# Attention kernel: value products of a group of heads moved into one run behind the last exponential

## The reference, cut to what matters

```
for 8 images of 512 tokens, width 256, 16 heads, latent width 32:
q_lat, k_lat, v_lat = projections of x to 32 latents a head; rotary on q_lat, k_lat
q_for_k = q_lat @ wqk.T + b
att = softmax(causal(q_for_k @ k_lat.T * 32**-0.5))     # 512 x 512 a head
y = (att @ v_lat) @ l2o.T + b ;  x = layernorm(x + y @ cproj.T + b)
# then: a soft mixture of 16 experts over 64 slots each, residual, layernorm
```

## Time and profile before

| | |
|---|---|
| runs | 1212.70, 1214.39, 1215.88 us; median 1214.39 |
| span of the profiled execution | 1212.4 us |
| TensorE matmul busy | 1152.4 us, 95% |
| VectorE, ScalarE, POOL busy | 769.8 (63%), 667.7 (55%), 596.1 (49%) |
| mask on POOL [L699] | 128 times, 748 ns in the mean |
| value products [L1439] | 1024 matmuls |

### The profile page before, as it was taken

How to read it: one execution, slowest core, us unless ns; L and a number is a source line. 1 busy time by engine, 2 the same in 40 slices (tenths; PEclk the granted TensorE clock), 3 DMA queues, 4 the chain that set the end, 5 groups by cost and what they waited for, 6 DMA issues and landing times.

```text
span 1212.4 us, 19086 instructions
## 1 busy us (share of the span) xinstructions
PE 1152.4 (95%) x6838; PEld 900.5 (74%) x6870; DVE 769.8 (63%) x1250; ACT 667.7 (55%) x946; POOL 596.1 (49%) x400
## 2 busy tenths in 40 slices
PE   6799999999999999998799999988999999999996
PEld 5566666666666666656688888867888888889885
DVE  5778796969686878654667667754544545522444
ACT  2456456665656565647779777755555555630112
POOL 6456565565656565612666666663444444440000
PEclk8799999999999999989899999998999999999998
DMA  4546454556555463630144335356654455364761
GB/s 142 125 111 155 95 132 94 145 120 158 124 127 147 99 161 89 184 108 1 53 157 157 122 122 183 105 165 234 183 166 148 160 163 182 113 213 144 246 234 53
DMA packets 126670, 170.29 MB, mean 140 GB/s; under 512 B 47041, under 2 KB 77186, under 8 KB 126594
## 3 DMA queue, kind: packets, MB, share of 16 engines
q1 hardware_dynamic: 124498, 168.74, 48.2%
q10 hardware_dynamic: 2096, 0.56, 0.2%
HBM read 72.26 MB, written 37.75 MB: 91 GB/s over the span
## 4 chain that ended last, share of the span: by engine, by line
PE 87%; DVE 6%; issue 2%; DMA 2%; ACT 1%; POOL 1%; SPq 1%; ACTq 1%; another core or an unknown queue 1%; DVEq 0%; POOLq 0%
PE ring L431 12%; PE ring L433 11%; PE ring L432 11%; PE ring L1428 7%; PE ring L1578 7%; PE tail L1439 7%; PE ring L1413 6%; PE tail L431 4%; PE tail L432 4%; PE tail L433 4%; PE ring L1461 2%; PE tail L1399 2%; PE tail L1578 2%; PE ring L1415 2%; PE ring L1515 2%
## 5 line engine op out<-in xcount | busy, mean ns | idle before, releaser
L1131 DVE TENSOR_REDUCE mx<-ring 128x4 f32<-128x512 f32 (+2 forms) x192 | 199.3, 1044 | 89.4 <-PE ring L1415 73.1
L842 ACT ACTIVATE pt<-ring 128x1024 f32<-128x1024 f32 (+1 forms) x192 | 169.1, 881 | 117.9 <-PE ring L1428 117.8
L699 POOL TENSOR_SCALAR_AFFINE_SELECT pt<-pt 128x512 f32<-128x512 f32 x128 | 95.7, 748 | 215.1 <-ACT pt L842 215.1
L1413 PE MATMUL ring<-qks 96*128 96x384 f32 (+3 forms) x512 | 137.0, 357 | 7.1 <-DMA qks<-stg 4.8
L1428 PE MATMUL ring<-qks 98*128 98x256 f32 (+3 forms) x512 | 137.5, 372 | 5.8 <-DMA qks<-mts 4.1
L1428 PEld LDWEIGHTS ring<-qks 98*128 98x128 f32 x512 | 79.4, 194 | 71.7 <-issue 47.6
L716 POOL TENSOR_TENSOR dl<-e,dh 128x1024 fp32r<-128x1024 f32 x32 | 76.6, 2404 | 94.6 <-ACT e L913 94.6
L740 POOL TENSOR_TENSOR hl<-hid,hh 128x512 fp32r<-128x512 f32 x64 | 82.7, 1303 | 76.8 <-ACT hh L948 76.8
L1439 PE MATMUL tail<-pt,va 128*32 128x512 f32 (+3 forms) x1024 | 97.0, 451 | 6.6 <-issue 4.9
L1413 PEld LDWEIGHTS ring<-qks 96*128 96x128 f32 x512 | 92.7, 199 | 12.6 <-issue 5.1
L1249 DVE SCALAR_TENSOR_TENSOR hid<-ring,bias_e,gate 128x512 f32<-128x512 f32 x64 | 47.9, 748 | 81.5 <-ACT gate L942 52.2
(11 more groups left out here) (241 smaller groups left out, 3069.7 us busy)
## 6 DMA issues: line engine op xcount, KB each, us to landing
qks<-stg SPq DMA_DIRECT2D x384, 128.0 KB, 2.4
c_dram<-c2s SPq DMA_DIRECT2D x32, 512.0 KB, 5.0
c<-c_dram SPq DMA_DIRECT2D x32, 512.0 KB, 6.5
sl_dram<-sls SPq DMA_DIRECT2D x32, 256.0 KB, 3.4
wg<-in_wg SPq DMA_DIRECT2D x16, 512.0 KB, 5.7
wu<-in_wu SPq DMA_DIRECT2D x16, 512.0 KB, 6.4
wd<-in_wd SPq DMA_DIRECT2D x16, 512.0 KB, 7.1
sl<-sl_dram SPq DMA_DIRECT2D x16, 512.0 KB, 4.6
```

The lines of the kernel that those rows point to most:

```text
L699: nc.gpsimd.affine_select(out=m, in_=m, compare_op=ALU.is_ge, fill=0.0, base=0, pattern=[[0, GH], [1, P]], channel_multiplier=-1).then_inc ...
L842: nc.scalar.activation(pt[j % 2][:, h:h + heads, 0:n], heads_of(tile, heads, n), ACT.Exp, scale=SCALE).then_inc(empty, 1)
L1131: nc.vector.tensor_reduce(out=mx[:, g, h:h + heads, i], in_=heads_of(tile, heads, (i + 1) * P), axis=AX.X, op=ALU.max).then_inc(empty, 1)
L1413: nc.tensor.matmul(scores[:, h, :], qks[0:KS_ROWS, g, 0, h0 + h, i * P:(i + 1) * P], qks[0:KS_ROWS, g, 1, h0 + h, 0:n], start=(h == k), st ...
```

## The change

The value products of a group, which were issued one by one behind the exp units of their blocks, are all given the due time of the last exp unit (`PV_WITH`), so they follow each other. Exp units are spaced by 1.0 instead of 8/6 (`EXP_SLOTS`), masks with them. Every key block has a `pt` buffer of its own: `pt0` of 512 columns a head, `pt1` of 384, `pt2` of 256, `pt3` of 128; `pt2` lies where a gap and two constants lay, which move to the end. The computation is the same. The diff:

```
--- before.py
+++ after.py
@@ -29,7 +29,9 @@
 MAX_UNITS = ((0, 0, 4), (1, 0, 4), (2, 0, 2), (2, 2, 2), (3, 0, 2), (3, 2, 2))
 EXP_UNITS = ((0, 0, 2), (0, 2, 2), (1, 0, 2), (1, 2, 2), (2, 0, 4), (3, 0, 4))
 EXP_LAST = (1, 3, 4, 5)
+PV_WITH = (3, 3, 3, 3)
 UNIT_SLOTS = GROUP_SLOTS / len(MAX_UNITS)
+EXP_SLOTS = 1.0
 
 
 PE_AT = {"lat": -20.25, "wqk": -9.25, "max": 0.0, "neg": 11.0, "exp": 13.25, "v": 14.55, "pv": 15.75, "yT": 28.75, "yTT": 53.5, "cproj": 58.5, "wv": -12.2, "seT": 6}
@@ -51,14 +53,22 @@
             if name in ("lat", "wqk", "neg", "yT", "khi", "qhi", "y", "shuffle", "cos", "qlo", "negmax", "sin", "add", "klo", "stack", "place"):
                 for g in range(G):
                     add(SPAN * b + GROUP_SLOTS * g, (name, b, g))
-            elif name in ("max", "exp"):
+            elif name == "max":
                 for g in range(G):
                     for u in range(len(MAX_UNITS)):
                         add(SPAN * b + GROUP_SLOTS * g + UNIT_SLOTS * u, (name, b, g, u))
-            elif name in ("pv", "mask"):
+            elif name == "exp":
+                for g in range(G):
+                    for u in range(len(EXP_UNITS)):
+                        add(SPAN * b + GROUP_SLOTS * g + EXP_SLOTS * u, (name, b, g, u))
+            elif name == "mask":
                 for g in range(G):
                     for j in range(NT):
-                        add(SPAN * b + GROUP_SLOTS * g + UNIT_SLOTS * EXP_LAST[j], (name, b, g, j))
+                        add(SPAN * b + GROUP_SLOTS * g + EXP_SLOTS * EXP_LAST[j], (name, b, g, j))
+            elif name == "pv":
+                for g in range(G):
+                    for j in range(NT):
+                        add(SPAN * b + GROUP_SLOTS * g + EXP_SLOTS * EXP_LAST[PV_WITH[j]], (name, b, g, j))
             elif name in ("seT", "seh", "sel"):
                 for c in range(NC if b == 0 else 0):
                     add(0, (name, b, c))
@@ -194,15 +204,14 @@
     stg = [place(f"stg{i}", [P, 4, T], f32r) for i in range(2)]
     qks = place("qks", [P, G, 2, GH, T], f32r)
     mts = [place(f"mts{i}", [2 * GH * NT, P], f32r) for i in range(2)]
-    at[0] += 3 * KB
-    identb = place("identb", [P, P], bf16)
-    maskb = place("maskb", [P, GH, P], bf16)
+    pt2 = place("pt2", [P, GH, T - 2 * P], f32)
+    at[0] += 256
     wq = place("wq", [P, P], f32)
     bwq = place("bwq", [P, 1], f32)
     bv = place("bv", [P, C], f32)
     va = place("va", [P, NT, H, L], f32)
     temp_at = at[0]
-    pt = [place(f"pt{i}", [P, GH, T], f32) for i in range(2)]
+    pt = [place("pt0", [P, GH, T], f32), place("pt1", [P, GH, T - P], f32), pt2, place("pt3", [P, GH, P], f32)]
     ys = place("ys", [P, T], f32)
     ytok = place("ytok", [P, NT, C], f32)
     yT_ = place("yT_", [P, NC, T], f32)
@@ -231,6 +240,8 @@
     m2 = place("m2", [P, NS], f32)
     es = place("es", [P, NS], f32)
     res = place("res", [P, NS], f32)
+    identb = place("identb", [P, P], bf16)
+    maskb = place("maskb", [P, GH, P], bf16)
 
     at[0] = temp_at
     wn = place("wn", [P, 6, C], f32)
@@ -694,7 +705,7 @@
                         if unit[0] == j:
                             done = ("exp", b, g, u)
                             pool.wait_ge(pair_drained[slot(done)], fill_count(done))
-                    m = pt[j % 2][:, :, 0:P]
+                    m = pt[j][:, :, 0:P]
 
                     nc.gpsimd.affine_select(out=m, in_=m, compare_op=ALU.is_ge, fill=0.0, base=0,
                                             pattern=[[0, GH], [1, P]], channel_multiplier=-1).then_inc(masked, 1)
@@ -839,7 +850,7 @@
                     j, h, heads = EXP_UNITS[st[3]]
                     n = T - j * P
                     act.wait_ge(full, fill_count(st))
-                    nc.scalar.activation(pt[j % 2][:, h:h + heads, 0:n], heads_of(tile, heads, n), ACT.Exp, scale=SCALE).then_inc(empty, 1)
+                    nc.scalar.activation(pt[j][:, h:h + heads, 0:n], heads_of(tile, heads, n), ACT.Exp, scale=SCALE).then_inc(empty, 1)
                 elif name == "y":
                     g = st[2]
                     act.wait_ge(y_filled, group(b, g))
@@ -1436,7 +1447,7 @@
                         if g == 0:
                             pe.wait_ge(pair_drained[slot(("v", b))], fill_count(("v", b)))
                     for h in range(GH):
-                        last = nc.tensor.matmul(ybank[h * L:(h + 1) * L, j * P:T], va[:, j, g * GH + h, :], pt[j % 2][:, h, 0:T - j * P],
+                        last = nc.tensor.matmul(ybank[h * L:(h + 1) * L, j * P:T], va[:, j, g * GH + h, :], pt[j][:, h, 0:T - j * P],
                                                 start=(j == 0), stop=(j == NT - 1))
                     if j == NT - 1:
                         last.then_inc(y_filled, 1)
```

## The result

| kernel | median | ratio to before, 95% interval |
|---|---|---|
| before | 1213.55 us (4 runs) | |
| changed | 1245.19 us (4 runs) | 1.0263 [1.0239, 1.0286] |

The account below looks back on a forecast made before the run. TensorE was taken to bound attention at full clock; after the change VectorE and ScalarE would bind ahead of lat. Terms +27.6, +3 and +1 sum to +31.6 us; on 1214.4 us the forecast was 1245 us, range 1222 to 1266.

Parts of the forecast that it names:

- images 1 to 6: Attention in these six images, counted from 0: 4.6 us slower an image, +27.6 us together.
- image 7 and what follows: Last image, no further lat steps to hide the last mask: +1 us, between -3 and +4.
- The front: Group from exp.0 to lat: bound by VectorE and ScalarE, lat at 8.7 us instead of 9.10, 0.4 gained.
- The tail: Group from lat to the next exp.0: gains value products, loses exp.5, 4.98 to 6.26 us, +1.3.
- fixed 0.15: TensorE time in us of each value product besides its columns; some two thirds of three (0.29) go in a run.
- border: End of an isolated value product on TensorE: removing one saves 0.29 us, between 0.22 and 0.37; three go per group.
- Ordinary: Attention group without v, apply, yTT or cproj: 14.1 to 15.0 us, +0.9.
- With apply: Attention group with v and ScalarE's apply: front +0.1, tail +1.3, together +1.4 us.
- With cproj: Attention group with yTT and cproj: front 0, tail +1.3, +1.4 us with rounding; cproj from 9.35.
- Rival 4: TensorE's granted clock falls in attention, for a tenth of the time: some 30 us more, 1275 us; chance 0.08.
- (1): Attention: TensorE stays the bound, only the saved ends of value products count, -26 us, 1188 us; chance 0.11.
- (2): Attention up to lat: VectorE alone binds, qhi no link, lat at 8.2, +16, 1230 us; chance 0.15.

Follow-up runs that it names:

- e6_sin: Changed kernel with POOL's sin put back ahead of mask.1; 1238.26 us, 1.0215 of before.
- e10_one: Changed kernel put back to the order of before, with only pv.2 moved to pv.3, behind max.4; 1210.55 us, 0.9975 of before.
- e8_half: Changed kernel with y, qhi back ahead of exp.2, sin ahead of mask.1, row maxima over the first half of columns only; 1205.34 us, 0.9958 of before.
- e4_run: Changed kernel with exp units spaced as before, keeping the run of four value products behind max.3; 1224.54 us, 1.0087 of before.
- e7_both: Changed kernel with ScalarE's y and qhi back ahead of exp.2 and POOL's sin back ahead of mask.1; 1230.28 us, 1.0150 of before.
- e1_pairs: Changed kernel put back to the order of before, but pv.0 with pv.1 behind neg, pv.2 with pv.3 behind max.4; 1205.04 us, 0.9920 of before.
- e9: Changed kernel in the order of before, value products paired behind neg and max.4, qhi behind exp.2 on ScalarE; 1207.51 us, 0.9935 of before.

## Why the prediction was right

**The sum.** By the starts of exp.0, the terms came out so:

| term | forecast | measured |
|---|---|---|
| ahead of the first exp.0 | none | +0.3 |
| images 1 to 6 | +27.6 | +24.3 |
| image 0 | +3 | +3.2 |
| image 7 and what follows | +1 | +6.6 |
| span | +31.6 | +34.4 |

The agreement of 1245.0 with 1245.2 is partly luck: one term was 3 too large and one 6 too small, and the span differs by 2.8.

**The front.** `lat` was forecast at 8.7, measured 9.2. The chain exp.2, y, qhi, qlo, negmax, max.1, lat is right in its order, and its durations to 0.2; khi made it start about 0.6 later. The step that failed is "khi on ScalarE and klo follow by 15.4. Next to need them: the next wqk": next to need khi was ScalarE itself, whose exp.0 stands behind it. In the group after one with cproj, add took 3.35 us instead of 2.39, since it started beside VectorE's `xtl` (446.34 to 447.71), and khi came 0.85 into the next group:

```profile
446.61 3.35 POOL L696 TENSOR_TENSOR rope<-rope,rot 128x1024 f32<-128x1024 f32 x1
```

e6_sin removes khi's wait, and `lat` moves from 9.2 to 8.6.

**The tail.** Forecast 6.26, measured 464.61 - 458.43 = 6.18. What stays of the fixed 0.15 between value products in a row: nothing. TensorE's weight loads, the run of four and the step behind it:

```profile
461.93 0.16 PEld L1450 LDWEIGHTS tail<-pt,va 128*32 128x32 f32 x8
...
464.22 0.42 PEld L1457 LDWEIGHTS tail<-ident,ys 128*128 128x128 f32 x4 [0.20 <-issue]
```

2.29 us for the four, against 0.99 + 0.78 + 0.57 + 0.36 = 2.70 one by one: 0.14 for each of three borders. The 0.12 ahead of a value product is there too (0.16 ahead of the run). The 0.10 behind it is less sure: I took it from `lat`'s first matmul, and that takes 0.33 here as well (458.43 to 458.76), with no value product ahead of it. exp.0 reaches max.4 in 0.54 behind yT (449.23 to 449.77) and took 0.58 behind pv.2, which leaves 0.04. So a border is worth between 0.30 and 0.36 to TensorE; I had taken 0.29. A group got less of it: 0.16 for the one border of e10_one. The Trainium skill (TensorEngine Tiling (Array Packing), Key Properties) says that changing the tiling mode drains the TensorE; the trace agrees, at 0.30 to 0.36 us for a value product that stands alone between full-width steps. That the drain is what takes this time is not shown: `neg` is 128x32 too, and in e8_half `lat` starts 0.03 behind it (431.19, 431.22).

**The groups.** Ordinary +0.9: measured +1.1 and +1.3. With apply +1.4: +1.15. With cproj +1.4: +0.84; there cproj began at 8.98, by ScalarE's exp.4, not 9.35. The size of each is off by up to 0.6, the sum of the image (+4.6) by 0.1 for image 5. That images 1 to 6 grew by only 24.3 has several causes, which the forecast did not have: image 6's last group, with no `lat` in it, took 12.64 before and 13.02 after; in images 2 and 4 of before the last group took 14.73 and 15.51, since exp.0 of the next waited for neg's transfer; and against that the clock fell once in the changed kernel:

```profile
365.05:381.82 16.77, 15.35 (x98) 10.41 (x96) 14.10 (x21) 9.25 (x13) 9.14 (x7) 0.90 0.48 120
434.02:449.23 15.21, 13.80 (x98) 9.33 (x96) 14.03 (x21) 8.49 (x12) 8.40 (x6) 1.00 0.34 78
```

These are the same group of images 4 and 5; the first holds a stretch at half clock and is 1.56 us longer. The longest wait of TensorE ahead of the fall there was 0.83 us.

**The last image.** I had +1 between -3 and +4; it was +6.6, outside these bounds, and this is the term that was mis-sized most. Rival 4 came about here and in the one group above. Busy time by stretch over `v` and over cproj of the last image:

```profile
533.40:537.80 4.40, 4.33 (x23) 4.33 (x24) 0.00 (x0) 4.40 (x10) 2.79 (x2) 0.61 0.00 0
557.30:562.60 5.30, 5.30 (x18) 4.40 (x18) 0.91 (x1) 0.60 (x1) 0.71 (x2) 0.64 0.40 120
```

The granted clock is 0.61 and 0.64 in the mean (half, 1.2 GHz, for most of the stretch), and `v` takes 4.35 us for 2.86, cproj 5.09 for 3.34 (first to last matmul): 3.2 of the 6.6 in these two steps alone. Before, the clock was full in both groups and fell only in the image's third, which took 14.1 before and 13.6 after. Ahead of `v`, TensorE had waited for exp.0's slot, 1.3 us, behind khi and the add. What makes the clock fall was not isolated: before, a wait of 1.27 us ahead of the same image (at 502.50) was followed by no fall.

**The rivals.** TensorE did not stay the bound (1). VectorE alone (2) is what e4_run shows: 1224.5, against 1230 forecast for it. The rest of the loss, 21 us, comes with the closer packing; both moves of e7_both give 15 of them back. The 5.7 us by which e7 is still above e4 are not in the ordinary run of groups: images 1 to 6 take 392.9 and 393.2. In the profiled executions e7's last image takes 48.0 us from its first exp.0 to its last against 42.1; its second and third group take 19.2 and 13.8 at a granted clock of 0.82 and 0.75, those of e4 17.6 at 0.90 and 9.9 at 1.00.

## What to carry over

An engine that is 99% busy bounds the kernel only in the order it has: work moved off one stretch is saved there only as far as the other engines' chains through that stretch allow, and it is paid in full where it lands. Before moving work, lay out the fixed chain of the other engines over the stretch (here seven links) and see how much it shortens; here 2.5 us of TensorE's work left the front and it became no shorter. Price the whole order of every engine with its slots, the in-order step ahead of a reader (khi ahead of exp.0) included, and let small gains be taken where cover remains: pairs (e1_pairs) came out 0.8% under before, part of it by the clock, and are with e9 the fastest of these kernels that keep the whole computation.

## What the runs showed of the hardware

VectorE operations with two SBUF inputs (cos, negmax) don't run beside POOL's. In the groups of VectorE's time, 60 to 530 us of the changed kernel:

```profile
L1132 DVE TENSOR_TENSOR rope<-lat,cos 128x1024 f32<-128x1024 f32 x28 | 68.0, 2428 | 0.0
L1152 DVE SCALAR_TENSOR_TENSOR negmax<-mx,negmax 128x16 fp32r<-128x16 f32 x28 | 13.6, 487 | 1.0
L1150 DVE SCALAR_TENSOR_TENSOR negmax<-mx,zeros 128x16 fp32r<-128x16 f32 x28 | 4.6, 166 | 0.0
```

`cos` takes 2.43 us in the mean, where it took 1.22, since `sin` moved behind mask.1 and runs when cos starts. POOL's timeline of the same group:

```profile
457.18 2.37 POOL L691 TENSOR_TENSOR rot<-rot,sin 128x1024 f32<-128x1024 f32 x1
459.51 2.21 POOL L710 TENSOR_SCALAR_AFFINE_SELECT pt<-pt 128x512 f32<-128x512 f32 x2
```

sin ends at 459.55; cos (458.30 to 460.64) ends 1.09 later, a little under the 1.22 that it takes alone, and the first of two masks that take 0.64 each starts beside it and the two take 2.21. The shuffle (451.77, 1.30 us), with one SBUF input, ran beside POOL's klo and mask.0 and took no longer. With `sin` back in its place (e6_sin) cos takes 1.38 in the mean. The Trainium skill (SBUF — State Buffer, SBUF: two separate sides) says that a VectorE operation with two SBUF inputs and a GpSimd operation that reads SBUF lock a shared pair of ports, the one that starts first for its whole length, while the other blocks; these rows agree. In the changed kernel cos has slack ahead of max.3, so its own 1.2 us cost VectorE nothing; but it holds up the masks by 0.9, and `xtl` the add by another 1.0, and behind these khi came late. negmax lies on the chain to `lat`: its two operations take 0.65 in the mean, where they took 0.54 before, so little of the loss is theirs.
